# Attention reads x1 in SBUF instead of reloading it; the recurrence's input in four buffers; the maxima's row on partition 127

## The chip, the core and the metric

The kernel runs on one core of a Trainium2 chip. The metric is the device time of one execution in microseconds (us), the median of several runs. The profile is one further execution, recorded instruction by instruction. Engines: PE is TensorE (matmuls; PEld is its weight load), DVE is VectorE, ACT is ScalarE, POOL is GpSimd, SP is SyncE, which only issues DMA transfers.

## What is computed

One layer: `x1 = x + mLSTM-like recurrence(layernorm(x))`, then `x2 = x1 + ffn(layernorm(x1))`, where ffn is a causal attention block with 16 heads followed by a top-2 mixture of 8 experts. x is 32 sequences of 256 rows of 128 numbers.

```python
x = x + _L0_attn_ref(_layernorm(x), W, b, input_bias, scale)      # the recurrence: scan over t
#   m = max(f+m, i); c = f_s*c + i_s*tanh(z); n = f_s*n + i_s; h = sigmoid(o)*c/n; rms-normed
x = x + _L0_ffn_ref(_layernorm(x), w_qkv, w_o, g1, b1, wg, w1, bb1, w2, bb2, g2, b2)
#   scores = q k / sqrt(8), causal; attn = softmax(scores); h = layernorm(x + attn v w_o)
#   top-2 of softmax(h wg); y = sum of two experts gelu(h w1 + bb1) w2 + bb2; layernorm(h + y)
```

## The kernel before

**Tiling.** The recurrence works in 16 groups g of two sequences (512 rows, one tile `cell.X[:, g % 3]`, `a_X` in the trace, 256 KB). Attention works in 32 blocks b of one sequence each. After both come the experts (71 tiles) and the combination of the results; the change doesn't touch these.

**Steps.** `layers` runs recurrence and attention as one software pipeline. Each engine has its own written order of work, `step(s)`, s from -5 to some forty. In a step, attention block s has its row statistics taken (`rows_stats` on DVE), block s-1 is normalised, projected to queries and keys and sent through a DRAM scratch into the layout of `QK` (`c_QK`), blocks s-2 and s-3 have the row maxima of their scores computed (`maximum` on PE, `reduce` on DVE, 12 of each per block), block s-4 gets its scores and exponentials (`score` on PE, `exp` on ACT), and so on. A recurrence group takes two steps for each stage. The phase of the group is fixed by the step's parity: `cell_stats` of group (s+5)/2 is in odd steps, near the head of DVE's step, after `rows_shift`. Engines execute strictly in the written order, and an instruction that waits holds up all that is behind it on its engine.

**SP's queue** issues in `step(s)`, in this order: in even steps the load of recurrence group s/2+3 (L491); the load of x1 of block s from DRAM into `X` (`b_X`, L518); the row of maxima of block s-3 (L522); three stores of queries and keys of block s-1 to scratch (L529, L530, L532); in odd steps the store of x1 of a group (L536); a row of zeros (L541), which waits until PE has done the twelve scores of the block that held this third of `QK`; and four loads from scratch into `QK` (L547), 768 KB, all on the same queue.

**Where x1 comes from.** POOL adds the recurrence's output to x in place, in `cell.X` (L610). SP stores that to DRAM, and attention reads it back 128 KB per block (`b_X`): `rows_stats` (L1347) and `rows_norm` (L857) read it there. The later stages read the DRAM copy too.

**Maxima.** `QK` holds, on the partition axis, four blocks of 24 of the 32 partitions. The key side `QK[:, n, 0:4]` is otherwise zero and the query side `QK[:, n, 4]` is one. The negated maxima are written on partition 24 of the key side, so that a `score` matmul over all 128 partitions subtracts them. A `maximum` matmul must not see them, and therefore the zeros are written over them before each refill. `score` matmuls wait for the row of maxima, `maximum(b, 0)` for the refill of `QK`: the four loads and the zeros.

Of the kernel before, what the change touches and what calls it, by code (L numbers as in the profile page):

```python
# [106 lines left out]
def cell_memory(nc):  # L107

    cell = Cell()
    with ExitStack() as ctx:  # L110
# [17 lines left out]
        cell.X = sb("a_X", [P, NC, 4, D])  # L128
# [20 lines left out]
        cell.r_rms = sb("a_r_rms", [P, 4])  # L149
    return cell  # L150
# [5 lines left out]
M_ROW = ROWS  # L156
# [6 lines left out]
NC = 3  # L163
NX = 3
# [46 lines left out]
def layers(nc, dram, const, kept):  # L211

    x1_t = dram["x1"].rearrange("(b t p) d -> b p t d", p=P, t=2)
# [6 lines left out]
    with ctx:  # L220
# [3 lines left out]
        def sem(name):  # L224
            return ctx.enter_context(nc.semaphore(name))
# [16 lines left out]
        zero_row = sb("b_zero", [HEADS, T])  # L242
        X = sb("b_X", [P, NX, 2, D])
# [116 lines left out]
        s_x = [sem(f"b_x{k}") for k in range(NX)]  # L360
# [95 lines left out]

        def stored(engine, g):

            engine.wait_ge(c_out[g % NC], 16 * (g // NC) + 16)

# [15 lines left out]
        WRITES, READS = 3 * 16, 5 * 16  # L476
        BROWS = 2 * E + 4
        FILLED = 3 + 2 * NQ
# [10 lines left out]
        def _(sync):  # L489
# [18 lines left out]
            cell_rows(2)  # L508

            def step(s):  # L510
                if s.base % 2 == 0 and NC <= s.base // 2 + NC < GROUPS:
                    stored(sync, s.base // 2)
                    cell_rows(s.base // 2 + NC)
                if s.exists(B):
                    b, n = s, s.of(NX)
                    need(sync, s_xn, b - (NX - 1))
                    stored(sync, b.base // 2)
                    sync.dma_start(X[:, n], x1_t[bass.ds(b.value(), 1)].rearrange("b p t d -> p (b t) d")).then_inc(s_x[n], 16)  # L518
                if (s - 3).exists(B):
                    b, n = s - 3, (s - 3).of(NQ)  # L520
                    need(sync, s_mtc, b + 1)
                    sync.dma_start(QK[M_ROW:M_ROW + 1, n, 0:NJ].rearrange("o j g n -> o (j g) n").bitcast(fp32), mt[:, :].bitcast(fp32)).then_inc(s_mr[n], 16)  # L522
                if (s - 1).exists(B):

                    b, n = s - 1, (s - 1).of(NQ)
                    need(sync, s_qkhi, b + 1)
                    need(sync, s_qkr[n], b.turn(NQ) * READS)
                    slots = scr[n].rearrange("s p n -> p s n")
                    sync.dma_start(slots[:, 0:4:3], qk_hi[:, :, :].bitcast(fp32)).then_inc(s_qkw[n], 16)  # L529
                    sync.dma_start(slots[:, 1:6:4], qk_hi[:, :, :].bitcast(fp32)).then_inc(s_qkw[n], 16)  # L530
                    need(sync, s_qklo, b + 1)
                    sync.dma_start(slots[:, 2:5:2], qk_lo[:, :, :].bitcast(fp32)).then_inc(s_qkw[n], 16)  # L532
                x = group(s, 4)
                if x.exists(GROUPS):
                    need(sync, c_x1, x + 1)
                    sync.dma_start(out_t[:, 4 * x.base:4 * x.base + 4, :], cell.X[:, x.of(NC)]).then_inc(c_out[x.of(NC)], 16)  # L536
                if (s - 1).exists(B):
                    need(sync, s_s, (b - NQ) * 12 + 12)
                    if b.base < NQ:
                        sync.wait_ge(s_fill, FILLED - 2 * (NQ - 1 - n))  # L540
                    sync.dma_start(QK[M_ROW:M_ROW + 1, n, 0:NJ].rearrange("o j g n -> o (j g) n").bitcast(fp32), zero_row[:, :]).then_inc(s_qkr[n], 16)  # L541
                if (s - 1).exists(B):
                    b, n = s - 1, (s - 1).of(NQ)
                    need(sync, s_qkw[n], b.turn(NQ) * WRITES + WRITES)
                    rows = scr[n].rearrange("(a s) (r j g) n -> j (s r) a (g n)", a=2, g=NG, j=NJ)
                    for j in range(NJ):
                        sync.dma_start(QK[32 * j:32 * j + ROWS, n, j:NJ + 1:NJ - j].rearrange("p a g n -> p a (g n)").bitcast(fp32), rows[j]).then_inc(s_qkr[n], 16)  # L547

            for s in range(GROUND, STEPS_B):
                step(Count(s))  # L550
                if B - 2 <= s < B + 2:
                    for e in range(2 * (s - B + 2), 2 * (s - B + 2) + 2):
                        sync.dma_start(kept["w1_f"][:, e, :], dram["w1"][e]).then_inc(s_w1, 16)
# [144 lines left out]
        def _(act):  # L698
# [4 lines left out]
            def weights():  # L703
# [7 lines left out]
                act.wait_ge(s_fill, 3)  # L711
# [140 lines left out]
            def rows_norm(a):  # L852
# [137 lines left out]
        def _(dve):  # L990
# [500 lines left out]
        def _(pe):  # L1491
# [105 lines left out]
            def maximum(b, u):  # L1597
# [639 lines left out]
```

## Time and profile before

| | us |
|---|---|
| median of 3 runs (1061.05 to 1064.22) | 1063.59 |
| the profiled execution | 1061.42 |
| its span, first to last instruction | 1059.6 |
| PE busy in the span | 902.4 |
| DVE busy | 849.5 |
| ACT busy | 769.8 |
| POOL busy | 535.0 |

The profiled execution is 2.2 us under the median of the runs. The span has four stretches: up to about 90 us the recurrence alone fills the pipeline, from 90 to some 650 us recurrence and attention run together, then attention drains and routing ends, and from about 720 us on the experts and the combination run. In a timeline row the first number is the start in us, the second how long the instruction or the merged run of instructions took, `x` how many there are, and in brackets stand the idle time before it and what ended that.

### The profile page before, as it was taken

The numbers are of one execution on the slowest core, as the hardware profiler recorded it, in microseconds if no ns is written. First come the engines' busy times: TensorE is split into PE (matmuls) and PEld (weight loads), VectorE is DVE, ScalarE is ACT, GpSimd is POOL, SyncE is SP. The second block draws the span as 40 slices with busy tenths as digits, with TensorE's granted clock in tenths as the row PEclk, the third lists the DMA queues.
The fourth block names the chain that finished last, engine by engine and source line by source line (L and its number), as shares of the span: only waits on it lengthen the run. The fifth ranks groups of instructions, "written<-read, shape, count | busy, mean of one in ns | idle before, by whom it ended". The sixth has DMA issues, their size and how long they took to land. (4 is left out here: it accounts for less than half of the span.)

```text
span 1059.6 us, 26142 instructions
## 1 busy us (share of the span) xinstructions
PE 902.4 (85%) x6922; PEld 698.3 (66%) x6922; DVE 849.5 (80%) x2533; ACT 769.8 (73%) x1905; POOL 535.0 (50%) x781
## 2 busy tenths in 40 slices
PE   1446899999999999999999998846999999999474
PEld 0234667676766766766676666536999999999421
DVE  4667989999999999998989888673777777777378
ACT  2776799999999999997897766751656656666356
POOL 8000243344356556656577767782555656656400
PEclk9657999999999999998999999965999999999788
DMA  1015543444354454545344556153333332332186
GB/s 52 1 51 130 132 108 108 113 118 111 90 136 118 120 128 118 136 108 124 104 127 126 137 140 160 40 119 102 88 99 86 92 89 85 95 86 67 48 247 190
DMA packets 138118, 114.69 MB, mean 108 GB/s; under 512 B 19459, under 2 KB 126601, under 8 KB 138005
## 3 DMA queue, kind: packets, MB, share of 16 engines
q1 hardware_dynamic: 120916, 92.24, 33.9%
q0 software_dynamic: 8640, 16.93, 5.0%
q10 hardware_dynamic: 8448, 4.20, 1.4%
q8 instruction: 48, 0.79, 0.3%
q14 instruction: 66, 0.53, 0.2%
HBM read 60.60 MB, written 52.58 MB: 107 GB/s over the span
## 5 line engine op out<-in xcount | busy, mean ns | idle before, releaser
L621 POOL TENSOR_SCALAR_AFFINE_SELECT b_PT<-b_PT 128x256 f32<-128x256 f32 (+1 forms) x384 | 191.0, 512 | 207.2 <-ACT b_PT L811 202.1
L1180 DVE TENSOR_REDUCE b_m_neg<-b_ps_m 128x2 f32<-128x512 f32 (+1 forms) x384 | 255.1, 681 | 33.9 <-PE b_ps_m L1615 15.8
L811 ACT ACTIVATE b_PT<-b_ps_s 128x512 f32<-128x512 f32 x384 | 219.6, 598 | 28.3 <-PE b_ps_s L1591 13.9
L1923 POOL DMA_INDIRECT results<-e_Y,e_X x142 | 151.7, 1068 | 121.4 <-DVE e_Y L1991 98.5
L656 POOL DMA_INDIRECT slots<-c_pay,b_pos x128 | 130.3, 1018 | 39.9 <-issue 36.5
L2039 PE MATMUL e_ps_d<-e_h,e_w 128*128 128x256 f32 x568 | 134.5, 380 | 0.0
L1615 PE MATMUL b_ps_m<-c_QK 128*128 128x256 f32 x512 | 123.3, 322 | 0.0
L1594 PE MATMUL b_ps_s<-c_QK 128*128 128x512 f32 x256 | 111.0, 434 | 5.6 <-ACT b_PT L811 5.4
L1950 ACT ACTIVATE e_h<-e_ps,e_w 128x256 f32<-128x256 f32 x284 | 111.3, 480 | 0.8 <-PE e_ps L2030 0.8
L2039 PEld LDWEIGHTS e_ps_d<-e_h,e_w 128*128 128x128 f32 x568 | 102.6, 191 | 11.0
L1943 ACT ACTIVATE e_yt<-e_ps_d,e_w 128x256 f32<-128x256 f32 x71 | 33.7, 475 | 99.2 <-PE e_ps_d L2039 99.2
L1965 DVE CAST e_w<-c_w1s 128x1024 fp32r x71 | 49.4, 696 | 67.6 <-PE e_ps L2030 66.2
L2028 PE MATMUL e_ps<-e_x_hi,e_w 128*128 128x256 f32 x284 | 93.9, 330 | 0.9 <-DVE e_x_lo L1970 0.9
L1608 PE MATMUL b_ps_m<-c_QK 128*128 128x128 f32 x512 | 94.3, 314 | 0.0
L1627 PE MATMUL b_ps_o<-b_PT,b_V 128*32 128x256 f32 x1024 | 82.7, 395 | 1.1 <-POOL b_PT L621 1.1
L1608 PEld LDWEIGHTS b_ps_m<-c_QK 128*128 128x128 f32 x512 | 79.7, 197 | 3.8
L2030 PE MATMUL e_ps<-e_x_hi,e_w 128*128 128x256 f32 x284 | 80.7, 284 | 0.0
L2029 PE MATMUL e_ps<-e_x_lo,e_w 128*128 128x256 f32 x284 | 80.5, 283 | 0.0
L1615 PEld LDWEIGHTS b_ps_m<-c_QK 128*128 128x128 f32 x512 | 79.6, 196 | 0.5
L1612 PE MATMUL b_ps_m<-mask_b,ident_b 128*128 128x256 bf16 x256 | 72.0, 281 | 6.9 <-DVE b_m_neg L1180 6.6
L1605 PE MATMUL b_ps_m<-mask_b,ident_b 128*128 128x512 bf16 x128 | 50.4, 394 | 26.4 <-DMA c_QK<-qk_scr 20.9
L610 POOL TENSOR_TENSOR a_X<-a_Y,a_X 128x512 f32<-128x512 f32 x16 | 20.5, 1281 | 89.1 <-DVE a_Y L1145 89.1
(253 smaller groups left out, 2311.6 us busy)
## 6 DMA issues: line engine op xcount, KB each, us to landing
c_QK<-qk_scr SPq DMA_DIRECT2D x128, 192.0 KB
qk_scr<-b_qk_hi SPq DMA_DIRECT2D x64, 256.0 KB
e_X<-slots SPq DMA_DIRECT2D x71, 130.0 KB, 2.3
qk_scr<-b_qk_lo SPq DMA_DIRECT2D x32, 256.0 KB
f_G<-results SPq DMA_DIRECT2D x32, 256.0 KB, 3.6
a_X<-in_L_attn_x_dram SPq DMA_DIRECT2D x16, 256.0 KB, 6.4
x<-a_X SPq DMA_DIRECT2D x16, 256.0 KB, 2.8
b_X<-x SPq DMA_DIRECT2D x32, 128.0 KB, 5.7
```

The source lines that it names most:

```text
L621: nc.gpsimd.affine_select(out=tri, in_=tri, compare_op=ALU.is_ge, fill=0.0, base=0, pattern=[[0, tri.shape[1]], [1, P]], channel_multiplie ...
L656: nc.gpsimd.indirect_dma_start(dram["slots"][:, :], bass.IndirectOffsetOnAxis(pos[:, q % NPOS, k, i:i + 1], 0), pay[:, r, t, k, :], None). ...
L811: nc.scalar.activation(PT[:, g % 2, q % 3], ps_s[:, q % 2], ACT.Exp, scale=HD ** -0.5).then_inc(s_e, 1)
L1180: nc.vector.tensor_reduce(out, scores, AX.X, ALU.max, negate=True).then_inc(s_red, 1)
L1594: nc.tensor.matmul(ps_s[:, q % 2].rearrange("p (j q) -> p j q", j=2), QK[:, n, NJ, g, 0:P], QK[:, n, 2 * u - 2:2 * u, g, :], start=True, s ...
L1608: done = nc.tensor.matmul(ps_m[:, u % 2, j * P:(j + 1) * P], QK[:, n, j, u, 0:P], QK[:, n, NJ, u, 0:P], start=False, stop=(j == 3), skip_g ...
L1615: done = nc.tensor.matmul(ps_m[:, u % 2, j * T:(j + 1) * T], QK[:, n, 2 * jp + j, g, P:T], QK[:, n, NJ, g, :], start=False, stop=(j == 1), ...
L1627: nc.tensor.matmul(ps_o[32 * j:32 * j + VW, g // 2, :], v_block(n, 0, g, j), PT[:, g % 2, 1 + j // 2, (j % 2) * T:(j % 2 + 1) * T], start= ...
L1923: nc.gpsimd.indirect_dma_start(dram["results"][:, :], bass.IndirectOffsetOnAxis(X[:, j.of(NB_X), u, D:D + 1].bitcast(u32), 0), Y[:, n, u, ...
L1950: nc.scalar.activation(h1[:, n, c], ps_1[:, c, 0:SUB * P], ACT.Gelu_apprx_tanh, bias=w2[:, n, F + c:F + c + 1]).then_inc(s_g, 1)
L2028: nc.tensor.matmul(out, w1[:, n, 1, col], x_hi[:, n], start=True, stop=False)
L2039: last = nc.tensor.matmul(ps_d[:, 0:SUB * P], w2[:, n, c * D:(c + 1) * D], h1[:, n, c], start=(c == 0), stop=(c == NF - 1))
```

## The change

- `b_X` is gone: no loads of x1 from DRAM for attention (32 transfers of 128 KB). `rows_stats` and `rows_norm` read `cell_row(b, t)`, a view of `cell.X`; `rows_stats` waits on `c_x1`, POOL's sum, instead of a DMA.
- `cell.X` has four buffers instead of three. Groups 0 to 3 are loaded ahead of the loop. Group g from 4 on is loaded in step 2(g-3), as before, but at the end of SP's step, after the four `QK` loads, instead of at its head. It waits until the store of group g-4 is done and until ACT has normalised both attention blocks of group g-4.
- The row of maxima lies on partition 127 (`M_ROW`), and a `maximum` matmul contracts over partitions 0 to 119 (`KEYS`) instead of 128, so that it doesn't see it. The zero rows are gone from SP's queue (32 transfers of 16 KB), as is their source and POOL's memset of it.
- SP's step is written as functions; the stores and the four `QK` loads stay in their order. The low part's store has one more wait, already met.

```diff
-NC = 3
-NX = 3
+NC = 4
-M_ROW = ROWS
+KEYS = 32 * (NJ - 1) + ROWS
+M_ROW = 127
...
+        def cell_row(b, t):
+
+            return cell.X[:, b.base // 2 % NC, 2 * (b.base % 2) + t, :]
...
-        WRITES, READS = 3 * 16, 5 * 16
+        WRITES, READS = 3 * 16, 4 * 16
...
             cell_rows(2)
+            cell_rows(3)
+
+            def recurrent_in(s):
+                g = s.base // 2 - 1 + NC
+                if s.base % 2 or not NC <= g < GROUPS:
+                    return
+                stored(sync, g - NC)
+                need(sync, s_xn, Count(2 * (g - NC) + 2))
+                cell_rows(g)
...
+            def operands(b):
+                if not b.exists(B):
+                    return
+                n = b.of(NQ)
+                need(sync, s_qkw[n], b.turn(NQ) * WRITES + WRITES)
+                need(sync, s_s, (b - NQ) * 12 + 12)
+                if b.base < NQ:
+                    sync.wait_ge(s_fill, FILLED - 2 * (NQ - 1 - n))
+                rows = scr[n].rearrange("(a s) (r j g) n -> j (s r) a (g n)", a=2, g=NG, j=NJ)
+                for j in range(NJ):
+                    sync.dma_start(QK[32 * j:32 * j + ROWS, n, j:NJ + 1:NJ - j].rearrange("p a g n -> p a (g n)").bitcast(fp32), rows[j]).then_inc(s_qkr[n], 16)
...
             def step(s):
-                if s.base % 2 == 0 and NC <= s.base // 2 + NC < GROUPS:
-                    stored(sync, s.base // 2)
-                    cell_rows(s.base // 2 + NC)
-                if s.exists(B):
-                    b, n = s, s.of(NX)
-                    need(sync, s_xn, b - (NX - 1))
-                    stored(sync, b.base // 2)
-                    sync.dma_start(X[:, n], x1_t[bass.ds(b.value(), 1)].rearrange("b p t d -> p (b t) d")).then_inc(s_x[n], 16)
...
+                maxima_row(b1)
+                columns_high(a)
+                columns_low(a)
+                recurrent_out(x)
+                operands(a)
+                recurrent_in(s)
...
-                    sync.dma_start(QK[M_ROW:M_ROW + 1, n, 0:NJ].rearrange("o j g n -> o (j g) n").bitcast(fp32), zero_row[:, :]).then_inc(s_qkr[n], 16)
...
-                    last = nc.scalar.activation(XN[:, a.of(NB), t, 0:D], X[:, a.of(NX), t, :], ACT.Identity,
+                    last = nc.scalar.activation(XN[:, a.of(NB), t, 0:D], cell_row(a, t), ACT.Identity,
...
-                k = n.of(NX)
-                need(dve, s_x[k], n.turn(NX) * 16 + 16)
+                need(dve, c_x1, Count(n.base // 2 + 1))
...
-                        done = nc.tensor.matmul(ps_m[:, u % 2, j * P:(j + 1) * P], QK[:, n, j, u, 0:P], QK[:, n, NJ, u, 0:P],
+                        done = nc.tensor.matmul(ps_m[:, u % 2, j * P:(j + 1) * P], QK[0:KEYS, n, j, u, 0:P], QK[0:KEYS, n, NJ, u, 0:P],
```

SP's queue before, in step 4 (even) up to the head of step 5. `a_X` is recurrence group 5, `b_X` x1 of an attention block, `b_mt` the row of maxima; what a transfer waits for stands in brackets (`b_s` counts scores, `b_qkw0` scratch stores, `a_out2` stores of x1).

```order
L491 DMA a_X<-in_L0_attn_x_dram 128x4x128 [waits a_out2]
L518 DMA b_X<-x1 128x2x128 [waits a_out2,b_xn]
L522 DMA c_QK<-b_mt 1x16x256 [waits b_mtc]
L529 DMA qk_scr<-b_qk_hi 128x2x256 [waits b_qkr0,b_qkhi]
L530 DMA qk_scr<-b_qk_hi 128x2x256
L532 DMA qk_scr<-b_qk_lo 128x2x256 [waits b_qklo]
L541 DMA c_QK<-b_zero 1x16x256 [waits b_s]
L547 DMA c_QK<-qk_scr 24x2x1024 [waits b_qkw0]
L547 DMA c_QK<-qk_scr 24x2x1024 x3
L518 DMA b_X<-x1 128x2x128 [waits a_out2,b_xn]
```

The same step after the change:

```order
L524 DMA c_QK<-b_mt 1x16x256 [waits b_mtc]
L533 DMA qk_scr<-b_qk_hi 128x2x256 [waits b_qkr0,b_qkhi]
L534 DMA qk_scr<-b_qk_hi 128x2x256
L543 DMA qk_scr<-b_qk_lo 128x2x256 [waits b_qkr0,b_qklo]
L561 DMA c_QK<-qk_scr 24x2x1024 [waits b_s,b_qkw0]
L561 DMA c_QK<-qk_scr 24x2x1024 x3
L491 DMA a_X<-in_L0_attn_x_dram 128x4x128 [waits b_xn,a_out1]
```

The load of group 5 moved from the head of SP's step 4 to its end, which is where the load of `b_X` for step 5 stood.

DVE's queue before, at the head of step 5 (odd), where the statistics of group 5 are taken (`a_stats`) between the shift of a block and the recurrence's scan; `a_x2` counts the landing of the load above.

```order
L1315 SCALAR_TENSOR_TENSOR b_shift<-b_means,b_roots 128x2 [waits b_xn,b_roots_s]
L1023 BN_STATS a_stats<-a_X 128x6 [waits a_mv_s,a_x2]
L1023 BN_STATS a_stats<-a_X 128x6 x3
L1075 SCALAR_TENSOR_TENSOR a_M<-a_sp,a_i 128x256 [waits a_us,a_it,a_sp_s]
L1075 SCALAR_TENSOR_TENSOR a_M<-a_sp,a_i 128x256
L1180 TENSOR_REDUCE b_m_neg<-b_ps_m 128x2 [waits b_b_s]
```

The same place after the change (group 5 is then in buffer 1):

```order
L1339 SCALAR_TENSOR_TENSOR b_shift<-b_means,b_roots 128x2 [waits b_xn,b_roots_s]
L1047 BN_STATS a_stats<-a_X 128x6 [waits a_mv_s,a_x1]
L1047 BN_STATS a_stats<-a_X 128x6 x3
L1099 SCALAR_TENSOR_TENSOR a_M<-a_sp,a_i 128x256 [waits a_us,a_it,a_sp_s]
L1099 SCALAR_TENSOR_TENSOR a_M<-a_sp,a_i 128x256
L1204 TENSOR_REDUCE b_m_neg<-b_ps_m 128x2 [waits b_b_s]
```

Nothing moved on DVE; the order on PE, DVE and ACT is the same before and after throughout.

## Rows read from the trace of the kernel before

**Rows 1.** The page, engines over the span, and granted clock in 40 slices

```profile
PE 902.4 (85%) x6922; PEld 698.3 (66%) x6922; DVE 849.5 (80%) x2533; ACT 769.8 (73%) x1905; POOL 535.0 (50%) x781
...
PEclk9657999999999999998999999965999999999788
```

**Rows 2.** One stretch: busy PE, PEld, DVE, ACT, POOL, clock, DMA share, GB/s

```profile
90.00:641.00 551.00, 516.87 (x4541) 377.59 (x4541) 509.76 (x1415) 481.77 (x1159) 296.43 (x503) 0.99 0.47 120
```

**Rows 3.** Waits, us, times, longest: PE on QK loads; DVE on b_X (L518)

```profile
PE b_ps_m L1605 <- DMA c_QK<-qk_scr: 20.9, 18, 3.7
...
  DVE b_stats L1347: 0.2, 1
```

**Rows 4.** Timeline of SP's queue, first and last odd-step slots and one pair

```profile
98.66 1.55 SPq L547 DMA_DIRECT2D c_QK<-qk_scr  x4
...
202.22 0.51 SPq L541 DMA_DIRECT2D c_QK<-b_zero  x1
202.77 2.06 SPq L547 DMA_DIRECT2D c_QK<-qk_scr  x4
204.93 0.40 SPq L518 DMA_DIRECT2D b_X<-x  x1
...
221.91 1.64 SPq L547 DMA_DIRECT2D c_QK<-qk_scr  x4
223.60 0.39 SPq L491 DMA_DIRECT2D a_X<-in_L_attn_x_dram  x1
...
506.62 1.77 SPq L547 DMA_DIRECT2D c_QK<-qk_scr  x4
```

**Rows 5.** Timeline of DVE, heads of three odd steps

```profile
98.79 0.86 DVE L1023 BATCH_NORM_STATS2 a_stats<-a_X 128x6 f32<-128x128 f32 x4
...
204.16 0.86 DVE L1023 BATCH_NORM_STATS2 a_stats<-a_X 128x6 f32<-128x128 f32 x4
205.36 1.27 DVE L1075 TENSOR_TENSOR_SCAN a_M<-a_sp,a_i 128x256 f32<-128x256 f32 x2 [0.34 <-issue]
207.35 0.69 DVE L1180 TENSOR_REDUCE b_m_neg<-b_ps_m 128x2 f32<-128x512 f32 x1 [0.72 <-PE b_ps_m L1615]
...
509.41 0.86 DVE L1023 BATCH_NORM_STATS2 a_stats<-a_X 128x6 f32<-128x128 f32 x4
```

**Rows 6.** Issues, us to landing: at 223.6, 204.9 and 60.7; the page's median

```profile
a_X<-in_L_attn_x_dram SPq DMA_DIRECT2D x1, 256.0 KB, 6.2
...
b_X<-x SPq DMA_DIRECT2D x1, 128.0 KB, 5.6
...
a_X<-in_L_attn_x_dram SPq DMA_DIRECT2D x1, 256.0 KB, 2.9
...
a_X<-in_L_attn_x_dram SPq DMA_DIRECT2D x16, 256.0 KB, 6.4
```

**Rows 7.** Timeline of PE, maximum(b, 8) in the odd step after 204.16

```profile
208.93 0.28 PE L1612 MATMUL b_ps_m<-mask_b,ident_b 128*128 128x256 bf16 x1
```

**Rows 8.** Timeline of PE, the same piece of an even step, twice

```profile
229.30 0.39 PE L1605 MATMUL b_ps_m<-mask_b,ident_b 128*128 128x512 bf16 x1 [0.59 <-DMA c_QK<-qk_scr]
...
233.52 0.64 PE L1627 MATMUL b_ps_o<-b_PT,b_V 128*32 128x256 f32 x8
...
493.26 0.54 PE L1605 MATMUL b_ps_m<-mask_b,ident_b 128*128 128x512 bf16 x1 [2.09 <-DMA c_QK<-qk_scr]
...
500.47 0.64 PE L1627 MATMUL b_ps_o<-b_PT,b_V 128*32 128x256 f32 x8
```

**Rows 9.** PE in stretches of 2 us: busy, granted clock, DMA share, GB/s

```profile
498.00:500.00 2.00, 2.00 (x11) 0.50 0.15 42
...
662.00:664.00 2.00, 2.00 (x15) 0.50 0.00 0
```

**Rows 10.** Timeline of PE at half clock, 33 and 128 partitions contracted

```profile
62.67 0.76 PE L1516 MATMUL a_ps_r<-a_ones_r,a_bf_w 33*128 33x512 f32 x1 [1.49 <-DVE a_xt_lo L1049]
63.37 0.79 PE L1507 MATMUL a_ps_r<-a_xt_hi,a_w_lo 128*128 128x512 f32 x1
```

More of the change, by code:

```diff
@@ L127, in cell_memory @@
         cell.eps_rms = sb("a_eps_rms", [P, 1])
-        cell.X = sb("a_X", [P, NC, 4, D])
         cell.stats = sb("a_stats", [P, 4, 6])
@@ L149, in cell_memory @@
         cell.r_rms = sb("a_r_rms", [P, 4])
+        cell.X = sb("a_X", [P, NC, 4, D])
     return cell
@@ L359, in layers @@
         s_fill = sem("b_fill")
-        s_x = [sem(f"b_x{k}") for k in range(NX)]
         s_st = sem("b_st")
@@ new lines, in _, with maxima_row @@
+            cell_rows(3)
[6 more added lines that the diff above has]
+                cell_rows(g)
+            def maxima_row(b):
+                if not b.exists(B):
+                    return
+                n = b.of(NQ)
+                need(sync, s_mtc, b + 1)
+                sync.dma_start(QK[M_ROW:M_ROW + 1, n, 0:NJ].rearrange("o j g n -> o (j g) n").bitcast(fp32), mt[:, :].bitcast(fp32)).then_inc(s_mr[n], 16)
@@ new lines, in columns_high, with columns_low @@
+            def columns_high(b):
+                if not b.exists(B):
+                    return
+                n = b.of(NQ)
+                need(sync, s_qkhi, b + 1)
+                need(sync, s_qkr[n], b.turn(NQ) * READS)
+                slots = scr[n].rearrange("s p n -> p s n")
+                sync.dma_start(slots[:, 0:4:3], qk_hi[:, :, :].bitcast(fp32)).then_inc(s_qkw[n], 16)
+                sync.dma_start(slots[:, 1:6:4], qk_hi[:, :, :].bitcast(fp32)).then_inc(s_qkw[n], 16)
+            def columns_low(b):
+                if not b.exists(B):
+                    return
+                n = b.of(NQ)
+                need(sync, s_qklo, b + 1)
+                need(sync, s_qkr[n], b.turn(NQ) * READS)
+                slots = scr[n].rearrange("s p n -> p s n")
+                sync.dma_start(slots[:, 2:5:2], qk_lo[:, :, :].bitcast(fp32)).then_inc(s_qkw[n], 16)
@@ new lines, in recurrent_out @@
+            def recurrent_out(g):
+                if not g.exists(GROUPS):
+                    return
+                need(sync, c_x1, g + 1)
+                sync.dma_start(out_t[:, 4 * g.base:4 * g.base + 4, :], cell.X[:, g.of(NC)]).then_inc(c_out[g.of(NC)], 16)
+            def operands(b):
+                if not b.exists(B):
+                    return
+                n = b.of(NQ)
+                need(sync, s_qkw[n], b.turn(NQ) * WRITES + WRITES)
[5 more added lines that the diff above has]
+                    sync.dma_start(QK[32 * j:32 * j + ROWS, n, j:NJ + 1:NJ - j].rearrange("p a g n -> p a (g n)").bitcast(fp32), rows[j]).then_inc(s_qkr[n], 16)
@@ L1342, in rows_stats @@
                     return
-                k = n.of(NX)
-                need(dve, s_x[k], n.turn(NX) * 16 + 16)
+                need(dve, c_x1, Count(n.base // 2 + 1))
                 need(dve, s_mv, n)
                 for t in range(2):
-                    last = nc.vector.bn_stats(stats[:, t, :], X[:, k, t, :])
+                    last = nc.vector.bn_stats(stats[:, t, :], cell_row(n, t))
                 last.then_inc(s_st, 1)
@@ L1614, in maximum @@
                     for j in range(2):
-                        done = nc.tensor.matmul(ps_m[:, u % 2, j * T:(j + 1) * T], QK[:, n, 2 * jp + j, g, P:T], QK[:, n, NJ, g, :],
+                        done = nc.tensor.matmul(ps_m[:, u % 2, j * T:(j + 1) * T], QK[0:KEYS, n, 2 * jp + j, g, P:T], QK[0:KEYS, n, NJ, g, :],
                                                 start=False, stop=(j == 1), skip_group_check=True)
```

40 lines of the change are left out of this document (6 added, 34 removed).

## The prediction

> **What bounds the kernel now.** I read the page first, then stretches, then waits, then the timelines of SP, DVE and PE around one pair of steps. Over the span PE is busy 85% and DVE 80% [rows 1], but that is a mean over unlike stages. In the 551 us in which recurrence and attention run together, PE is busy 516.9, DVE 509.8 and ACT 481.8 us [rows 2], so 94, 93 and 87%: three engines in written orders, of which two have no room to take up a delay of several us. A stall of DVE there goes nearly whole into the time. A stall of a DMA counts only where an engine stands waiting for it. For the four QK loads PE does: 20.9 us in 18 waits. For the reload of x1 nobody does: 0.2 us, once [rows 3].
>
> **The reload of x1 goes.** It was hidden, so its removal gives 0.2 us. The same holds at the start of the pipeline, since the statistics of block 0 stand late in DVE's order and that one wait is all. What remains is less traffic, 4 MB of it. The new wait, on POOL's sum, is met a step earlier than DVE asks, and behind it on DVE nothing changes. I cost it at nothing; if the sum were late, DVE's whole step would wait.
>
> **The zero rows go.** They stand on SP's queue just before the QK loads and take the slot from 202.22 to 202.77 [rows 4]. The wait for PE's last score now falls on the first load, so the loads start 0.55 us earlier. One of the 18 waits, the longest with 3.7 us, is at the start, where the loads wait for the stores to scratch and the zeros don't matter. That leaves 17 waits of up to 0.55 us each, 9.4 us at most. Some are shorter than 0.55. I take 8 us off; bounds 4 and 13, the latter if the 2.09 us wait [rows 8] shrinks enough to spare the fall of the clock behind it.
>
> **Fewer partitions in the maxima.** 120 rows contracted instead of 128, 1024 matmuls. At one clock a matmul over 33 partitions takes 0.76 us and one over 128 takes 0.79 [rows 10]. The 0.03 us for 512 columns, a quarter to a half of it for the 128 and 256 columns here, would be some 0.01 us x 1024, 10 us either way at the very worst. I cost it at nothing, since even a quarter of the partitions moves the row by 4% only.
>
> **The load of the recurrence's input moves.** This is the step that decides. It stood at the head of SP's even step and now stands at its end, behind the four QK loads, one step (some 18 us) later. The statistics that need it are at the head of DVE's next step. Two views give how late it comes.
>
> 1. When DVE asks: at 204.16 in the pair shown [rows 5]. The slot of the load is that of `b_X` at 204.93, less the 0.55 us of the zeros, so 204.4 [rows 4]. It isn't even issued when DVE asks.
> 2. When it lands: behind the QK loads this very transfer took 6.2 us at 223.6, its median is 6.4, and half its size took 5.6 us in the slot at 204.9 [rows 6]. Counted from the first of the four loads, 223.60 - 221.91 = 1.7 us ahead of the issue [rows 4], the median gives 6.4 + 1.7 = 8.1 us. The first load would start at 202.22, where the zeros stood, so the input lands at 202.2 + 8.1 = 210.3, and DVE stands from 204.16 to 210.3: 6.2 us.
>
> The same sum for the other pairs needs the start of the first load and DVE's row. There are 12 such loads, groups 4 to 15. In the first, 98.66 against 98.79, the loads wait for the scratch stores, so no 0.55 comes off: 8.1 - 0.1 = 8.0 us. In the last, 506.62 against 509.41, it is 8.1 - 0.55 - 2.8 = 4.8 us [rows 4, 5]. The eleven after the first lie between these 4.8 and 6.5, mean 5.7.
>
> **What of that reaches the end.** In the pair shown DVE resumes at 210.3 and needs 0.86 + 1.27 + 0.69 = 2.8 us for the statistics, the scan and the reduction of maximum 6 [rows 5], so it is through at 213.1. PE's maximum 8 needs this one; it ran at 208.93 [rows 7]. PE therefore stops for 4.2 us. DVE itself loses 6.2 less the idle 0.34 and 0.72 us that it had there anyway [rows 5], so 5.1. Where the wait is shorter (4.8), DVE ran behind PE with about one us less between its row and maximum 8, and PE loses 3.9. I take PE's 4.2: 11 x 4.2 = 46 us, and 8 for the first, so 54; bounds 11 x 3.9 + 8 = 51 and 11 x 5.1 + 8 = 64. SP is held up by nothing in this: its two waits on the moved load are met earlier in the step.
>
> **The clock.** In the trace PE stood 2.09 us before 493.26, and then ran at the granted clock of 0.50, that is 1.2 GHz, for some 7 us. The same piece of work took 500.47 - 493.26 = 7.2 us against 233.52 - 229.30 = 4.2 at the full 2.4 GHz [rows 8, 9]: 3.0 us lost. Another stretch at 0.50 shows near 663 [rows 9]. Stops of 4.2 us are twice as long as that of 2.09, so I expect a fall at nearly each of the 12. Some of the half clock will lie in the stop itself, and DVE comes out of it about a microsecond behind PE, which hides as much. I take 2.0 of the 3.0 us each: 24 us; bounds 0 and 36.
>
> **Sum.** Against the profiled execution's 1061.4 us: + 54 + 24 - 8 = + 70, so 1131. That execution is 2.2 us under the median of the runs, so I forecast 1063.6 + 70 = 1134 us for the median.
>
> **Rivals.**
>
> *The clock holds.* Then the clock's 24 us fall away: 1063.6 + 54 - 8 = 1110. For it: one measured fall is thin evidence, and the 0.59 us wait left the speed alone [rows 8]. Against it: the fall after 2.09 us. Chance 17%.
>
> *The delay is DVE's and the fall a long one.* Each stop costs DVE's 5.1 and the full 3.0 us: 64 + 36 - 8 = + 92, 1156. It happens if the work after the stop, at half clock, is bound by PE throughout and nothing is caught up. Chance 14%.
>
> *The input isn't held up by the QK loads.* With SP's queue free the transfer landed in 2.9 us [rows 6]. Then DVE stands 204.4 + 2.9 - 204.16 = 3.1 us, PE 3.1 + 2.8 - 4.8 = 1.1 us, the clock holds, and the time is 1063.6 + 12 x 1.1 - 8 = 1069. The trace speaks against it: 6.2 us in a like place, and 5.6 for half the size. Beside this rival stands a sentence of the Trainium skill, "DMA: Bandwidth & Descriptors", section "Anatomy of one DMA": a transfer costs about 2.0 us and its bytes over 436 GB/s. For 256 KB that would be an estimate of 2.6 us, which agrees with the 2.9 of the free queue and not with the 6.2 and 6.4 behind 768 KB of other loads. Chance 4%.
>
> *Faster.* If the input were in place before DVE asks, only the 0.55 us of each QK load would remain, and perhaps one fall of the clock spared: 1063.6 - 8 - 3 = 1053. This needs the input at least 6 us sooner than reckoned, so a load that is issued ahead of the QK loads. It also covers the case that I place the slot a step wrong. Against it stands that the wait for ACT's normalisation of block s-1 can't be met before the same step. Chance 4%.
>
> *Same,* by partial effects that cancel: 1%.
>
> **How the numbers follow.** The forecast has the remaining 60%. The range reaches from the clock that holds, with 51 for the stall and 13 off (1063.6 + 38, and a little below for shorter landings), to the long fall with a margin: 1095 to 1165. It leaves out the last three cases and tails, some 12%. A measurement of this kernel can tell 0.3%, about 3 us, from no change. Faster by more: 0.04; within: 0.01; slower: 0.95.
>
> **What would show it.** In the profile after, DVE's first `a_stats` row of each odd step from 100 to 510 us should follow 5 to 6 us of idle time that ends with the DMA of `a_X`, 12 times and some 70 us in all. PE should stop 4 us before the maximum 8 behind it, with a granted clock of 0.50 after most of them and a mean clock below 0.93. The waits of PE on the QK loads should shrink from 20.9 to about 12 us. The pairs of steps should take 43 us instead of 37, up to the last load, and 37 after it. The time from 720 us on should be as before, only later. Wrong would be an `a_stats` row with no idle time before it, or an `a_X` that lands within 3 us.

## The result and the profile after

| | before | after |
|---|---|---|
| median, us | 1062.32 (1059.24 to 1064.22) | 1119.38 (1117.97 to 1122.55) |
| profiled execution / its span | 1061.42 / 1059.6 | 1122.55 / 1120.8 |
| PE, DVE busy in the span | 902.4, 849.5 | 923.8, 849.4 |
| mean granted clock | 0.937 | 0.915 |

Four runs of each; the ratio is 1.054, with a 95% interval of 1.051 to 1.058. The changed kernel is 57 us slower. The profiled execution after is the longest of its four, so the spans differ by a little more, 61.2 us. The forecast was 1134 in a range of 1095 to 1165.

First the page of the kernel after, the engines over the span and the granted clock in 40 slices (as [rows 1]), then the stretch of 90 to 641 us with the columns of [rows 2], which all engines now work through more slowly:

```profile
PE 923.8 (82%) x6884; PEld 716.7 (64%) x6922; DVE 849.4 (76%) x2533; ACT 770.8 (69%) x1905; POOL 543.0 (48%) x780
...
PEclk9656999989998989989999999995799999999888
```

```profile
90.00:641.00 551.00, 479.14 (x3953) 352.66 (x3983) 456.69 (x1255) 439.75 (x1047) 261.20 (x429) 0.93 0.37 97
```

PE does 37.7 us less work in these 551 us, DVE 53.1 less, at a mean clock of 0.93 instead of 0.99 [rows 2]. The waits (us, times, longest) name the reason:

```profile
DVE a_stats L1047 <- DMA a_X<-in_L_attn_x_dram: 68.0, 12, 7.6
...
PE b_ps_m L1635 <- DVE b_m_neg L1204: 56.7, 28, 7.3
...
PE b_ps_m L1631 <- DMA c_QK<-qk_scr: 8.5, 5, 3.0
```

The first row isn't in the kernel before at all. The second stood there with 6.6 us in 15 waits, and the third, at L1605, with 20.9 in 18 [rows 3]. So DVE waits for the recurrence's input, PE waits for DVE, and PE waits less for the QK loads than it did. One pair of steps shows it, SP first, then DVE, then PE:

```profile
220.44 2.72 SPq L561 DMA_DIRECT2D c_QK<-qk_scr  x4
223.26 0.39 SPq L491 DMA_DIRECT2D a_X<-in_L_attn_x_dram  x1
```

```profile
228.80 0.87 DVE L1047 BATCH_NORM_STATS2 a_stats<-a_X 128x6 f32<-128x128 f32 x4 [6.34 <-DMA a_X<-in_L_attn_x_dram]
229.59 1.26 DVE L1099 TENSOR_TENSOR_SCAN a_M<-a_sp,a_i 128x256 f32<-128x256 f32 x2
230.77 0.67 DVE L1204 TENSOR_REDUCE b_m_neg<-b_ps_m 128x2 f32<-128x512 f32 x1
```

```profile
226.79 0.47 PE L1617 MATMUL b_ps_s<-c_QK 128*128 128x512 f32 x1 [0.29 <-ACT b_PT L835]
231.49 0.39 PE L1635 MATMUL b_ps_m<-mask_b,ident_b 128*128 128x256 bf16 x1 [4.23 <-DVE b_m_neg L1204]
...
237.77 0.64 PE L1650 MATMUL b_ps_o<-b_PT,b_V 128*32 128x256 f32 x8
```

DVE asks at 222.5 (228.80 less the 6.34 of idle time), before the load is even issued at 223.26. It lands 5.5 us later. PE stands for 4.2 us and then works at half clock. From maximum 8 to the `b_ps_o` row it needs 6.28 us. The same piece of the kernel before, from the row at 208.93 [rows 7] to this one, took 4.04:

```profile
212.97 0.64 PE L1627 MATMUL b_ps_o<-b_PT,b_V 128*32 128x256 f32 x8
```

The granted clock, in stretches of 2 us of PE (busy, clock, DMA share, GB/s), shows two kinds of fall: a short one in the pair before and a long one in this pair.

```profile
188.00:190.00 2.00, 0.48 (x3) 0.80 0.00 0
190.00:192.00 2.00, 2.00 (x11) 0.50 0.00 0
192.00:194.00 2.00, 1.97 (x12) 0.85 0.00 0
...
230.00:232.00 2.00, 0.51 (x3) 0.54 0.02 4
...
234.00:236.00 2.00, 2.00 (x9) 0.50 0.00 0
236.00:238.00 2.00, 2.00 (x14) 0.76 0.00 0
238.00:240.00 2.00, 2.00 (x26) 1.00 0.00 0
```

There is such a fall at each of the 12 stops. The second and the last `a_stats` rows, which the sums below use:

```profile
144.82 0.87 DVE L1047 BATCH_NORM_STATS2 a_stats<-a_X 128x6 f32<-128x128 f32 x4 [6.01 <-DMA a_X<-in_L_attn_x_dram]
...
572.01 0.87 DVE L1047 BATCH_NORM_STATS2 a_stats<-a_X 128x6 f32<-128x128 f32 x4 [3.60 <-DMA a_X<-in_L_attn_x_dram]
```

The twelfth stands at 572.01 instead of 509.41, 62.6 us later, and the span ends 61.2 later. From the last load on nothing more is lost.

### The profile page after: what moved, and what is told of

It reads as the page before. It is cut to its first block and busy times, and to the rows that moved or that the text cites. A ratio compares the mean times of both kernels' runs of the same rounds, so it can differ in the third digit from the quotient of the medians.

```text
span 1120.8 us, 26083 instructions
## 1 busy us (share of the span) xinstructions
PE 923.8 (82%) x6884; PEld 716.7 (64%) x6922; DVE 849.4 (76%) x2533; ACT 770.8 (69%) x1905; POOL 543.0 (48%) x780
## 5 line engine op out<-in xcount | busy, mean ns | idle before, releaser
L645 POOL TENSOR_SCALAR_AFFINE_SELECT b_PT<-b_PT 128x256 f32<-128x256 f32 (+1 forms) x384 | 195.8, 524 | 252.4 <-ACT b_PT L835 246.9
L1638 PE MATMUL b_ps_m<-c_QK 120*128 120x256 f32 x512 | 135.7, 350 | 0.0
L1635 PE MATMUL b_ps_m<-mask_b,ident_b 128*128 128x256 bf16 x256 | 77.6, 303 | 57.0 <-DVE b_m_neg L1204 56.7
L1631 PE MATMUL b_ps_m<-c_QK 120*128 120x128 f32 x512 | 98.2, 322 | 9.3 <-DMA c_QK<-qk_scr 8.5
L1638 PEld LDWEIGHTS b_ps_m<-c_QK 120*128 120x128 f32 x512 | 89.3, 218 | 1.1
L1635 PEld LDWEIGHTS b_ps_m<-mask_b,ident_b 128*128 128x128 bf16 x256 | 25.9, 101 | 97.1 <-DVE b_m_neg L1204 72.9
L1631 PEld LDWEIGHTS b_ps_m<-c_QK 120*128 120x128 f32 x512 | 83.3, 205 | 4.3
```

What stands on the lines that cost most here:

```text
L645: nc.gpsimd.affine_select(out=tri, in_=tri, compare_op=ALU.is_ge, fill=0.0, base=0, pattern=[[0, tri.shape[1]], [1, P]], channel_multiplie ...
L1638: done = nc.tensor.matmul(ps_m[:, u % 2, j * T:(j + 1) * T], QK[0:KEYS, n, 2 * jp + j, g, P:T], QK[0:KEYS, n, NJ, g, :], start=False, stop ...
```

## The experiments

Eleven kernels ran, one of them twice. First the table, then each with what was expected.

| label | base and edit | median us | against before (95%) | DVE waits for a_X | PE waits for QK loads |
|---|---|---|---|---|---|
| e1_load_mid | after, load ahead of QK loads | 1053.3 | 0.989 (0.985 to 0.994) | 1.1 | 7.4 |
| e1b_load_mid_again | the same | 1053.5 | 0.991 (0.988 to 0.994) | 1.0 | 6.4 |
| e2_before_late | before, load at the end | 1136.1 | 1.067 (1.062 to 1.072) | 77.2 | 13.3 |
| e3_load_first | after, load just ahead of QK loads | 1059.2 | 0.995 (0.992 to 0.999) | 10.9 | 9.7 |
| e4_pe_filled | after, PE kept busy in the stops | 1111.1 | 1.043 (1.038 to 1.048) | 68.8 | 5.3 |
| e5_mid_zeros | e1, zero rows back | 1062.5 | 1.000 (0.997 to 1.002) | 1.1 | 14.9 |
| e6_mid_reload | e1, reload of x1 back | 1053.2 | 0.990 (0.987 to 0.993) | 1.0 | 7.1 |
| e7_mid_zeros_wide | e5, 128 partitions | 1062.9 | 1.001 (0.998 to 1.003) | 1.1 | 14.7 |
| e8_late_zeros | after, zero rows back | 1138.9 | 1.072 (1.067 to 1.077) | 76.6 | 15.6 |
| e9_late_reload | after, reload back | 1123.6 | 1.059 (1.053 to 1.064) | 70.4 | 9.2 |
| e10_head_and_out_last | after, SP's order changed further | 1052.2 | 0.991 (0.987 to 0.994) | none | 7.9 |
| e11_mid_zeros_ahead | e1, zero rows exactly as before | 1085.5, another chip | 1.004 (0.999 to 1.008) | 1.2 | 6.4 |

### e1_load_mid and e1b_load_mid_again: the load back ahead of the QK loads

```diff
                 columns_low(a)
+                recurrent_in(s)
                 recurrent_out(x)
                 operands(a)
-                recurrent_in(s)
```

> The changed kernel with one edit: the load of the recurrence's input stands right behind the three stores to scratch, ahead of the four QK loads, instead of behind them. All else of the change stays. My theory (the late load is the whole loss; everything else of the change costs nothing or gives back): DVE's a_stats rows of the odd steps don't wait for a_X any more (the 68.0 us are gone), PE doesn't stop before maximum 8, the granted clock stays at 1.00 between 100 and 510 us, and only the gain of the zero rows is left, 4 to 13 us: 1049 to 1059 us, 1054 at best guess, a ratio to before of 0.988 to 0.996. Rival (another part of the change costs time, such as the shared tile of x1, the four buffers' later release or the 120 partitions): the time stays well above before, over 1070.

> The same kernel as e1_load_mid, again, as the base of the three that follow and with more rounds, to see whether it beats the kernel before by more than the measurement is uncertain. Theory (the QK loads start 0.55 us earlier and that is the gain): 1053 us, 8 us under before, a ratio of 0.992. Rival (the first ratio of 0.989 was a good chip): within 0.3% of before.

1053.3 and 1053.5 us, where 1054 and 1053 were expected. One line moved takes back 66 us, and 9 more than the change had cost. The waits of e1_load_mid, of DVE and of PE:

```profile
PE b_ps_m L1628 <- DMA c_QK<-qk_scr: 7.4, 6, 3.1
PE b_ps_m L1635 <- DVE b_m_neg L1204: 6.9, 15, 1.1
...
DVE a_stats L1047 <- DMA a_X<-in_L_attn_x_dram: 1.1, 1, 1.1
```

The load is issued right behind the stores to scratch. In the page of e1_load_mid the input lands 3.0 us after its issue, against 5.9 in the kernel after. This kernel beats both: the rest of the change is a gain of 0.9%, with an interval of 0.6 to 1.2%. The late load is the whole loss. One thing came out otherwise than expected: in e1_load_mid the clock fell once between 100 and 510 us, from 112 to 115; in e1b_load_mid_again it didn't.

### e2_before_late: the late load alone, in the kernel before

```diff
             def step(s):
-                if s.base % 2 == 0 and NC <= s.base // 2 + NC < GROUPS:
-                    stored(sync, s.base // 2)
-                    cell_rows(s.base // 2 + NC)
...
                         sync.dma_start(QK[32 * j:32 * j + ROWS, n, j:NJ + 1:NJ - j].rearrange("p a g n -> p a (g n)").bitcast(fp32), rows[j]).then_inc(s_qkr[n], 16)
+                if s.base % 2 == 0 and NC <= s.base // 2 + NC < GROUPS:
+                    stored(sync, s.base // 2)
+                    cell_rows(s.base // 2 + NC)
```

> The kernel before with one edit: the load of the recurrence's input is moved from the head of SP's even step to its end, behind the four QK loads. The reload of x1 for attention, the zero rows and the 128 partitions stay. My theory: this edit alone makes the loss, without the 8 us that the zero rows give and with DVE's wait 0.5 us longer at most: 12 waits of a_stats for a_X, 68 to 75 us together, and 1122 to 1134 us. Rival (it takes the change's other parts, since the reload of x1 takes a slot between the QK loads and the next input): under 1110. Second rival (the place of the load doesn't matter): 1062.

1136.1 us, 2 over the range, and the wait of 77.2 us is 2 over its range as well. That the mechanism is right shows in its 12 times, here in its row. Why the size was too small is what e8 asks.

```profile
DVE a_stats L1023 <- DMA a_X<-in_L_attn_x_dram: 77.2, 12, 8.1
```

### e3_load_first: late in issue, but with nothing ahead of it in the queue

```diff
-                operands(a)
-                recurrent_in(s)
+                operands(a, s)
...
                     sync.wait_ge(s_fill, FILLED - 2 * (NQ - 1 - n))
+                recurrent_in(s)
                 rows = scr[n].rearrange("(a s) (r j g) n -> j (s r) a (g n)", a=2, g=NG, j=NJ)
```

> The changed kernel with one edit: the load of the recurrence's input is issued after SP has waited for the stores to scratch and for PE's scores, but ahead of the four QK loads. It is issued as late as in the changed kernel less the 1.7 us of the four issues, but no bytes are queued ahead of it. If it is the 768 KB ahead that make the landing late (what my prediction says), the input lands within some 3 to 4 us of its issue instead of 6, DVE waits 1 to 3 us instead of 5.7, and the 12 stops of PE shrink to 0 to 1 us without a fall of the clock: 1060 to 1075 us, QK loads slightly later. If the landing takes 6 us in this place whatever stands ahead (the engines of the DMA busy with other queues' transfers), only the 1.7 us are won: 12 x 1.7 = 20 us and some of the clock, 1090 to 1105. If the moment of issue alone decides: above 1110.

1059.2 us, a little better than the range given for the theory. SP's queue in one pair, and then, from the page's table of transfers, the median from issue to landing:

```profile
205.20 0.37 SPq L491 DMA_DIRECT2D a_X<-in_L_attn_x_dram  x1
205.63 1.86 SPq L563 DMA_DIRECT2D c_QK<-qk_scr  x4
```

```profile
a_X<-in_L_attn_x_dram SPq DMA_DIRECT2D x16, 256.0 KB, 3.2
```

In this pair the load is issued at 205.20 and DVE starts its statistics at 208.41. The input is issued just as late in the step as the QK loads and lands within 3.2 us. DVE waits 10.9 us in 10 waits, not 68.0 in 12. The clock fell at the first stop only, where DVE waited longest, 3.0 us; it was 0.50 until about 115 us. So of the 5.9 us of the landing in the kernel after, 2.7 are the 768 KB ahead of it on its queue, and the issue of those four loads puts it back by another 1.7. The Trainium skill, "DMA: Bandwidth & Descriptors", section "Queues, rings and completion order", says that each DMA engine takes the descriptors of one issuing engine's queue in order. The trace agrees: 3.2 us ahead of the 768 KB, 5.9 behind. The estimate of 2.6 us that the prediction took from that page's section "Anatomy of one DMA" is 0.4 to 0.6 short of the 3.0 and 3.2 of e1 and e3. That section gives its figures for transfers that GpSimd issues, which the prediction left out, while this load is issued by SP; and they don't describe a transfer with others ahead of it.

### e4_pe_filled: the stop with PE kept busy

```diff
+FILL = 14
...
+            def filler(s, c):
+                if not c.exists(B) or not 3 <= s.base <= 25:
+                    return
+                need(pe, s_e, 12 * c + 2)
+                for _ in range(FILL):
+                    nc.tensor.matmul(ps_s[:, 1], cell.w_hi[:, 0:D], cell.xt_hi[:, :], start=True, stop=True)
...
                     score(c, 2)
+                    filler(s, c)
                     maximum(b1, 8)
```

> The changed kernel with work added to PE: ahead of maximum 8 in the 12 odd steps whose a_stats wait, 14 matmuls of 128 by 512 whose results are overwritten by the next score and never read (the output is as before). At 0.2 us each they fill 3 us of PE's stop of some 4. It tells what the clock costs. If the clock costs 2.0 us a fall, as predicted, and these keep it at 1.00, the time falls by 20 to 24 us to 1095 to 1100. If the fall costs 1 to 1.5 us, as the rows after the stops suggest, it falls by 6 to 15 us. If the clock costs nothing, or if it falls all the same, the time stays or grows by up to 12 x 0.3 us.

1111.1 us, 8.3 under the kernel after: the middle case of the three, a fall that costs 1 to 1.5 us. PE's timeline in the pair that was shown for the kernel after, and its clock in the same columns as above:

```profile
227.60 3.53 PE L1626 MATMUL b_ps_s<-a_xt_hi,a_w_hi 128*128 128x512 f32 x14 [0.96 <-ACT b_PT L836]
230.97 0.28 PE L1643 MATMUL b_ps_m<-mask_b,ident_b 128*128 128x256 bf16 x1
...
235.20 0.64 PE L1658 MATMUL b_ps_o<-b_PT,b_V 128*32 128x256 f32 x8
```

```profile
230.00:232.00 2.00, 1.91 (x12) 1.00 0.00 0
...
234.00:236.00 2.00, 2.00 (x27) 1.00 0.00 0
```

The clock stays at 1.00. The piece from maximum 8 to `b_ps_o` takes 4.23 us, not 6.28. The filler itself isn't quite free. In the kernel after, maximum 8 begins 0.72 us after the start of the reduction that it waits for (231.49 less 230.77). In e4 that reduction begins at 229.88, so maximum 8 was due at 230.60 and came 0.37 late:

```profile
229.88 0.67 DVE L1205 TENSOR_REDUCE b_m_neg<-b_ps_m 128x2 f32<-128x512 f32 x1
```

The same reading gives 0.4 to 0.65 us of lateness in six of the ten pairs from the second stop on, 3.4 us in all, none in the other four, and 1.6 us at the last stop.

The pair as a whole: between two `a_stats` rows, with the wait at the end taken off, the kernel after needs from 228.80 to 270.95 less 4.64, so 37.5 us, and this one from 227.92 to 269.50 less 5.76, so 35.8, 1.7 less. These are the rows of the kernel after and of e4:

```profile
270.95 0.87 DVE L1047 BATCH_NORM_STATS2 a_stats<-a_X 128x6 f32<-128x128 f32 x4 [4.64 <-DMA a_X<-in_L_attn_x_dram]
```

```profile
227.92 0.87 DVE L1048 BATCH_NORM_STATS2 a_stats<-a_X 128x6 f32<-128x128 f32 x4 [6.06 <-DMA a_X<-in_L_attn_x_dram]
...
269.50 0.87 DVE L1048 BATCH_NORM_STATS2 a_stats<-a_X 128x6 f32<-128x128 f32 x4 [5.76 <-DMA a_X<-in_L_attn_x_dram]
```

Worked out in this way for the ten intervals from the second stop on, the two kernels differ by 9.9 us, 1.0 for each fall: 1.3 on the mean for the five long ones (0.50 for some 7 us), 0.7 for the five short ones (some 3.5 us). If the filler's lateness of 3.4 us reached the end in full, it would be 13.3 us, 1.3 for each. So a later fall costs 1.0 to 1.3 us. The first stop has no filler, since no block has scores yet: the 154 matmuls more on PE (7076 against 6922) are eleven times 14, not the twelve that were meant. PE stood for 6.76 us there and the clock fell, until about 125 us:

```profile
108.30 0.40 PE L1643 MATMUL b_ps_m<-mask_b,ident_b 128*128 128x256 bf16 x1 [6.76 <-DVE b_m_neg L1205]
```

```profile
120.00:122.00 2.00, 2.00 (x11) 0.50 1.02 322
122.00:124.00 2.00, 2.00 (x9) 0.50 0.58 155
124.00:126.00 2.00, 2.00 (x9) 0.53 0.76 166
126.00:128.00 2.00, 2.00 (x27) 1.00 0.53 113
```

### e5, e6, e7: the parts of the change with the load in its early place

Of e5 and e6 only the main lines are shown. The counts of the semaphores, the declarations and POOL's memset of the zero row belong to them, and in e6 the normalisation on ACT reads `X` too.

e5_mid_zeros:

```diff
+                sync.dma_start(QK[M_ROW:M_ROW + 1, n, 0:NJ].rearrange("o j g n -> o (j g) n").bitcast(fp32), zero_row[:, :]).then_inc(s_qkr[n], 16)
                 rows = scr[n].rearrange("(a s) (r j g) n -> j (s r) a (g n)", a=2, g=NG, j=NJ)
```

> e1_load_mid with the row of zeros back on SP's queue ahead of the QK loads in each step (16 KB, 32 times, written to partition 127). All else as in e1_load_mid. My theory (the zero rows' slot of 0.55 us delays each QK load, at which PE waits): PE's waits on the QK loads go back to some 20 us, and the time up by 8 us (4 to 13) to 1057 to 1066. Rival (the gain comes from less traffic, since x1 isn't reloaded): unchanged within 2 us of e1b.

e6_mid_reload:

```diff
+                if s.exists(B):
+                    need(sync, s_xn, s - (NX - 1))
+                    stored(sync, s.base // 2)
+                    sync.dma_start(X[:, s.of(NX)], x1_t[bass.ds(s.value(), 1)].rearrange("b p t d -> p (b t) d")).then_inc(s_x[s.of(NX)], 16)
                 maxima_row(b1)
...
-                    last = nc.vector.bn_stats(stats[:, t, :], cell_row(n, t))
+                    last = nc.vector.bn_stats(stats[:, t, :], X[:, k, t, :])
```

> e1_load_mid with the reload of x1 back: 32 loads of 128 KB at the head of SP's step, and the row statistics and the normalisation of attention read the reloaded tile. My theory (it was hidden): within 2 us of e1b. Rival (its 4 MB and its slot on SP's queue delay the QK loads or the input): 3 to 8 us slower than e1b, and then e5_mid_zeros shows less than 8.

e7_mid_zeros_wide:

```diff
-KEYS = 32 * (NJ - 1) + ROWS
+KEYS = P
```

> e5_mid_zeros with the maximum matmuls over all 128 partitions again instead of 120 (the zeros make that right). My theory: within 2 us of e5_mid_zeros, as rows of 33 and 128 partitions differ by 4%. Bound: 1024 matmuls by 0.01 us, 10 us either way.

The zero rows cost 9.0 us (1062.5 against 1053.5) and take the whole gain away. PE's waits on the QK loads grow from 6.4 to 14.9 us, not to the 20 expected. That both numbers are near 9 doesn't make them the same microseconds: up to the last `a_stats` row e5 is only 1.9 us later than e1 and 2.8 later than e1b. The rest is lost behind it, where the clock fell three times in e5, for some 14 us of half clock, and once, for some 3, in each of e1 and e1b. Two of the three in e5:

```profile
640.00:642.00 2.00, 2.00 (x11) 0.50 0.13 37
...
660.00:662.00 2.00, 2.00 (x20) 0.50 0.00 0
```

How much of the 9 us is the slot of the row and how much the clock, no run separates. The reload of x1 costs nothing that can be measured (1053.2). Eight partitions more or less cost nothing either (1062.9 against 1062.5). The Trainium skill, "TensorE: Matmul & The Clock Gate", section "Step-by-step: what each phase is for", says of the weight load that its time goes by the columns and the number of rows doesn't matter. The trace agrees: the two groups of weight loads of the maxima take 200 and 197 ns on the mean over 120 partitions (e5) and 199 and 196 over 128 (e7). The matmuls take 317 and 325 ns against 316 and 323. PE's waits on the QK loads, of e5_mid_zeros, and DVE's wait on the reload, of e6_mid_reload:

```profile
PE b_ps_m L1634 <- DMA c_QK<-qk_scr: 14.9, 13, 4.0
```

```profile
DVE b_stats L1379 <- DMA b_X<-x: 0.3, 1, 0.3
```

### e11_mid_zeros_ahead: the zero rows in their exact place

```diff
-                need(sync, s_qkw[n], b.turn(NQ) * WRITES + WRITES)
                 need(sync, s_s, (b - NQ) * 12 + 12)
...
                 sync.dma_start(QK[M_ROW:M_ROW + 1, n, 0:NJ].rearrange("o j g n -> o (j g) n").bitcast(fp32), zero_row[:, :]).then_inc(s_qkr[n], 16)
+                need(sync, s_qkw[n], b.turn(NQ) * WRITES + WRITES)
```

> e5_mid_zeros wasn't an exact undo: its row of zeros stood behind the wait for the stores to scratch, while in the kernel before it stands ahead of that wait and behind the wait for PE's last score. There its slot costs nothing where the stores land last. Here the row has its place of before. The traces of e1 and e5 show 1.9 us of difference up to the last a_stats row and some 6 after it, where attention drains. If the wait for PE's last score comes last nearly always (as I reckoned), nothing changes: 1060 to 1063 us. If in the drain the stores land last, the row costs less: 1055 to 1058, and the kernel before loses the rest of its 8 us elsewhere, by the fall of the clock at 493 that e1 doesn't have.

It ran on a chip on which both kernels took 2% longer (1085.5, and 1084.5 before), so only the ratio counts: 1.0035, with an interval of 0.9994 to 1.0076. With its zero rows in the place of before, the kernel is as fast as before or a trifle slower, while without them it is at 0.991. So by the ratios the zero rows in either place cost some 9 us, or a little more, and the first of the two cases expected fits. The trace doesn't show it as a wait: PE waits 6.4 us for the QK loads, as in e1b without the zeros, where e5 has 14.9 and before 20.9. So where this kernel loses its time is open, and absolute times of that chip can't be set against the others. In the traces of e1 and e5, 1.9 us of it lie ahead of the last `a_stats` row and some 6 behind it. Between before and e1, 6.2 lie ahead of it, and 4.1 of these in the one interval in which before had the fall of the clock near 493 [rows 8, 9], which e1 hasn't: 42.92 us between the last two `a_stats` rows, against 38.81.

### e8_late_zeros and e9_late_reload: the parts again, with the late load

The edits are those of e5 and e6, made to the kernel after.

> The changed kernel (late load of the input) with the row of zeros back ahead of the QK loads. With the load of the input at its end, e2_before_late was 17 us slower than the changed kernel, not 8. It differs from it in the zeros, the reload of x1 and the 128 partitions. Theory now (the zeros count twice there: once at PE's waits on the QK loads, 8 us, and once more since the input's load, last in the queue, is pushed back by them too, 12 x 0.77 us of DVE's wait): 1132 to 1137 us, DVE's waits for a_X 75 to 79 us. Rival (the reload of x1 takes its part when the input is late): 1127, and the rest in e9_late_reload.

> The changed kernel (late load of the input) with the reload of x1 back at the head of SP's step and read by attention. Theory: as the changed kernel, 1117 to 1122 us, DVE's waits for a_X 66 to 71 us. Rival: the reload costs 8 us here, 1127, since it follows right behind the late input on the queue.

1138.9 us with the zeros, 2 over the range given, and 1123.6 with the reload. The first is 19.5 over the kernel after and more than accounts for e2's 16.7. Its waits:

```profile
DVE a_stats L1050 <- DMA a_X<-in_L_attn_x_dram: 76.6, 12, 8.4
...
PE b_ps_m L1634 <- DMA c_QK<-qk_scr: 15.6, 13, 3.9
```

The zeros make DVE's wait 8.6 us longer and PE's on the QK loads 7.1 us longer. The two add up to 15.7; e8's span is 14.6 us over that of the kernel after. So with a late load the same 16 KB count twice, as they push back both what PE waits for and what DVE waits for. Some of it can be the clock: eight of the eleven later falls are long in e8, and five in the kernel after. The reload is 4.2 us over in the medians, outside the 1117 to 1122 expected, but the two profiled spans are 1120.4 and 1120.8, and the intervals of the two ratios overlap. A cost of a few us isn't excluded; the 8 of the rival is not what the spans show.

### e10_head_and_out_last: are the last waits on the QK loads to be had?

```diff
+                recurrent_in(s)
                 columns_high(a)
                 columns_low(a)
-                recurrent_out(x)
                 operands(a)
-                recurrent_in(s)
+                recurrent_out(x)
```

> The changed kernel with the load of the input ahead of the stores to scratch of the same step, and with the store of x1 moved behind the QK loads. It asks whether PE's last waits on the QK loads (7.4 us in e1_load_mid) can be won as well. Theory (they are bytes ahead in the queue: 256 KB in each step, of the input or of x1's store): waits of 2 to 4 us, 1048 to 1051 us. Rival (the longest one, 3.1 us, is at the pipeline's start, and the others end when the stores to scratch have landed or PE's last score is done): 1052 to 1055, as e1_load_mid.

1052.2 us: the rival. PE still waits:

```profile
PE b_ps_m L1631 <- DMA c_QK<-qk_scr: 7.9, 6, 3.4
```

With no input and no store of x1 on the queue between the stores to scratch and the QK loads, nothing is won. e10 and e1 can't be told apart, and both beat the kernel before by 0.9%.

## Why the prediction was right, and where its sizes were off

**The mechanism is the one forecast.** DVE waits 12 times, once for each load from group 4 on, 68.0 us in all, where some 70 were forecast. PE stops behind it for 4.2 us in the pair shown, with the clock at 0.50 after each stop. The eleven later stops of PE last 2.6 to 4.9 us, 3.9 on the mean, and the first 7.3, where 4.2 and 8 were taken. e1 takes the late load away and 66 us go; e2 puts it into the kernel before and 75 come. e3 shows both parts of the lateness as reckoned: the issue behind the four QK loads, and the 768 KB ahead of the transfer.

**The stall: 54 forecast, 52 to 55.5 measured.** Between e1 and the kernel after, the twelfth `a_stats` row moves from 503.23 to 572.01, by 68.8 us. e4 splits this. At the first row e4 is 6.3 us later than e1 (105.61 against 99.30); 8.0 had been taken. In the ten intervals from the second stop on, with the clock at full speed, it loses 45.1 us to 55.3 us of waits: 1.0 us of each wait is made good, where I had taken 1.5 off (5.7 less 4.2). With the same 1.0 off the 6.0 us wait of the second stop, and 10.2 off the 54.3 us of the ten behind it, the stall is 6.3 + 5.0 + 44.1, so 55.5. Up to 3.4 of the 45.1 can be the filler's own lateness. Then the stall is 52 and the clock gets as much more. The rows of e1, the first, the second and the last, and of e4, the second and the last:

```profile
99.30 0.88 DVE L1047 BATCH_NORM_STATS2 a_stats<-a_X 128x6 f32<-128x128 f32 x4 [1.07 <-DMA a_X<-in_L_attn_x_dram]
...
130.02 0.86 DVE L1047 BATCH_NORM_STATS2 a_stats<-a_X 128x6 f32<-128x128 f32 x4
...
503.23 0.86 DVE L1047 BATCH_NORM_STATS2 a_stats<-a_X 128x6 f32<-128x128 f32 x4
```

```profile
145.95 0.87 DVE L1048 BATCH_NORM_STATS2 a_stats<-a_X 128x6 f32<-128x128 f32 x4 [6.20 <-DMA a_X<-in_L_attn_x_dram]
...
564.30 0.87 DVE L1048 BATCH_NORM_STATS2 a_stats<-a_X 128x6 f32<-128x128 f32 x4 [3.69 <-DMA a_X<-in_L_attn_x_dram]
```

**The clock: 24 forecast, 13 to 17 measured.** This is the term that was mis-sized. I took 2.0 us for each fall from one example in which the work lost 3.0. The falls came, all twelve. But a later fall costs 1.0 to 1.3 us on the mean, and only the first, which lasted from 104 to 117 us, costs more: its interval takes 39.20 us, against 30.72 of e1 and 5.0 for the stall, so 3.5. With the ten that sum to 9.9, that is 13.4 up to the last row, and 16.8 if the filler's lateness reached the end. Two things were missed. Six of the eleven later falls were half as long as the one in the trace of before. And the loss of a long fall isn't always that of the slow piece: the piece behind the stop loses 2.1 us in the pair shown (6.28 against 4.23 in e4) and the whole interval 1.7, or 2.1 with the 0.37 of the filler, so nothing need be made good there; but over the five long ones the mean is 1.3, or 1.6 with the filler's share. Whether other engines' slack takes up the rest no run shows.

**The zeros: -8 forecast, -8 to -9 measured, but not by the sum that gave it.** Spans of e1 and before differ by 8.3 us, and e5 over e1b is 9.0. The forecast spread the 8 over 17 waits of up to 0.55 us and kept the fall of the clock near 493; a spared fall stood only in its bound of 13. In the traces of before and e1 4.1 of the 8.3 us are the interval of that fall, and between e1 and e5 most lies behind the last load, where e5 has more falls. So that the size came out is in part luck. PE's waits on the QK loads fell from 20.9 to 8.5 us, further than the 12 forecast, and the zeros are only a part of it: e2 keeps them, with a late load, and has 13.3. That a row in front of a late load also makes that load later was in the sum for the landing (the 0.55 us that came off the slot), but it had not been seen as a second gain in the stall.

**Nothing for the reload and for the 120 partitions:** e6 and e7 agree within 0.4 us.

**The sum.** On spans 55.5 + 14 - 8.3 = 61.2, with 14 as the remainder (up to 17 with 52 for the stall); forecast 54 + 24 - 8 = 70. The median moved by 57. The range held it, and the nearest rival, with the clock that holds (1110), is close to what e4 came out at when the clock was held in all stops but the first: 1111.1.

**The other signs:** two `a_stats` rows are 41.7 to 43.6 us apart (39.2 at the first), where 43 was forecast. The mean clock is 0.915, forecast below 0.93. From the twelfth row to the end it takes 548.8 us, and 550.2 before.

## What to carry to other kernels

A transfer that nobody waits for has no price only in its place: before moving it, set its landing, counted from the first byte queued ahead of it, against the row that asks for it. Here a 256 KB load behind 768 KB on the same queue landed in 5.9 us instead of 3.0, and with its place a step later that cost 66 us, while the edit that looked like the saving, 4 MB less traffic, was worth nothing. A small transfer in front of one that an engine waits for has a price each time, here 9 us for 32 rows of 16 KB with the falls of the clock that came with them, and 19.5 where two waits end behind it. What a fall of the clock costs is to be read between two rows of the waiting engine, not in the slow piece alone; and a filler that holds the clock has to be checked for the time that it takes itself.

## What the runs showed of the hardware

At PE's later stops (2.6 to 4.9 us) the granted clock fell to 0.50, that is 1.2 GHz, for either some 3.5 or some 7 us, six times the one and five times the other. At the first stop, of 7.3 us, it fell within the stop and stayed there for 14 us (20 in e4, with a stop of 6.8), although PE worked again from 108 us on, in e4 with rows at 2.00 busy of 2.00. In e4, where 3.5 us of each later stop were filled with matmuls of no use, the clock stayed at 1.00 behind all eleven of them, and that was worth 8 us.
